# A Flamingo block on one core: key and value loads, the first normalisation and the shared FFN's matmul pieces moved in a hand-written order

## The reference

```python
x = x + tanh(g_xattn) * xattn(layernorm(x), ctx, ctx, W, b, mask)   # 16 heads of 16, causal and padding mask
z = layernorm(x)
shared = swiglu(z @ w_in.T) @ w_out.T                               # 256 -> 2 * 512 -> 256
# two groups of four experts: softmax over the groups, softmax in the best group, two best experts
h = swiglu(z @ w1.T)
routed = sum over experts e of (h * weight[:, e]) @ w2[e].T
x = x + tanh(g_ffn) * (shared + routed)
```

## Time and profile before

| | us |
|---|---|
| median of three runs | 1433.58 (1431.30 to 1433.97) |
| the profiled execution | 1430.63 |
| its span, first to last instruction | 1428.8 |
| mean granted TensorE clock | 0.929 of full speed |
| busy: TensorE, VectorE, GpSimd, ScalarE | 1201.9, 865.6, 552.0, 502.2 |

### The profile page before, as it was taken

The page is one execution under the profiler, slowest core; times in us unless marked ns, Lnnn a source line. Parts: engine busy times, 40 slices in busy tenths (PEclk is TensorE's granted clock), DMA queues, the critical chain, the costliest instruction groups (busy, mean ns, idle before and its releaser), DMA issues.

```text
span 1428.8 us, 22394 instructions
## 1 busy us (share of the span) xinstructions
PE 1201.9 (84%) x7387; PEld 953.1 (67%) x7387; DVE 865.6 (61%) x1968; ACT 502.2 (35%) x780; POOL 552.0 (39%) x658
## 2 busy tenths in 40 slices
PE   0577988888888888888888898626999999999997
PEld 0245766666666666666766666525888888888886
DVE  4435667466466567566466567773666666666665
ACT  3334434443444444444443443222222222222221
POOL 1112222422422422422522514354555656555543
PEclk9989999999999899999899899867999999999999
DMA  5466435445435335435435321343222222222210
GB/s 161 85 112 114 93 81 100 85 83 95 88 74 100 84 80 101 85 80 100 86 80 98 73 47 46 75 118 83 63 71 65 65 68 73 65 64 66 69 42 9
DMA packets 108263, 115.30 MB, mean 81 GB/s; under 512 B 36942, under 2 KB 88433, under 8 KB 108148
## 3 DMA queue, kind: packets, MB, share of 16 engines
q1 hardware_dynamic: 96376, 85.41, 29.1%
q0 software_dynamic: 11776, 28.46, 6.7%
HBM read 50.44 MB, written 28.64 MB: 55 GB/s over the span
## 4 chain that ended last, share of the span: by engine, by line
PE 57%; DVE 10%; DMA 8%; POOL 8%; issue 7%; SPq 5%; ACT 4%; POOLq 0%; ACTq 0%; DVEq 0%
PE ps L681 14%; PE ps L699 10%; DMA af<-in_ctxT 7%; PE ps L702 5%; PE ps L635 5%; PE ps L618 5%; POOL tab_dram L1375 3%; PE ps L541 3%; PE ps L526 3%; PE ps L550 3%; POOL gl L1358 2%; SPq L421 2%; PE ps L502 2%; PE ps L497 2%; PE ps L594 1%
## 5 line engine op out<-in xcount | busy, mean ns | idle before, releaser
L699 PE MATMUL ps<-w2a,gh 128*128 x608 | 218.7, 399 | 0.0
L702 PE MATMUL ps<-w2a,gl 128*128 x608 | 170.6, 281 | 0.0
L759 ACT ACTIVATE Pt<-ps,pbias 77x1024 f32<-77x1024 f32 x128 | 141.5, 1106 | 73.6 <-PE ps L528 73.1
L1358 POOL TENSOR_TENSOR gl<-gf,gh 128x512 fp32r<-128x512 f32 x64 | 82.6, 1290 | 148.1 <-ACT gh L801 148.1
L1303 POOL TENSOR_SCALAR ve<-mv 128x2 f32<-128x2 f32 x64 | 15.6, 244 | 317.0 <-DVE mv L882 316.4
L1411 POOL DMA_INDIRECT out<-ot,Pt x76 | 78.4, 1032 | 153.2 <-DVE ot L1232 149.7
L699 PEld LDWEIGHTS ps<-w2a,gh 128*128 128x128 f32 x608 | 114.3, 188 | 25.2
L681 PE MATMUL ps<-z2h,w1h 128*128 128x512 f32 x304 | 122.0, 401 | 7.4 <-DVE z2l L886 7.4
L618 PE MATMUL ps<-x2h,winh 128*128 128x512 f32 x256 | 124.3, 486 | 2.4 <-DVE gf L1157 1.5
L1093 DVE TENSOR_REDUCE mneg<-ps 128x8 f32<-128x616 f32 x128 | 101.6, 795 | 35.8 <-PE ps L502 35.7
L681 PE MATMUL ps<-z2l,w1h 128*128 128x512 f32 x304 | 121.1, 398 | 0.0
(11 more groups left out here) (205 smaller groups left out, 2858.7 us busy)
## 6 DMA issues: line engine op xcount, KB each, us to landing
w2a<-w2a SPq DMA_DIRECT2D x96, 256.0 KB, 5.8
af<-in_x SPq DMA_DIRECT2D x32, 256.0 KB, 4.1
x<-in_x SPq DMA_DIRECT2D x32, 256.0 KB, 7.0
y_dram<-xn SPq DMA_DIRECT2D x32, 256.0 KB, 3.5
y_dram<-res SPq DMA_DIRECT2D x32, 256.0 KB, 2.6
w2a<-w2a SPq DMA_DIRECT2D x96, 77.0 KB, 2.8
Pt<-in_w2T SPq DMA_DIRECT2D x16, 256.0 KB, 3.0
af<-in_ctxT SPq DMA_DIRECT2D x16, 154.0 KB, 6.8
```

The costliest lines, as they stand in the source:

```text
L699: e.matmul(o, gh2[:, c % 2, fc, t * P:(t + 1) * P], w2v[:, bass.ds(val, 1), fc, :, :].rearrange("p o h d -> p (o h) d"), start=fc == 0, st ...
L702: m = e.matmul(o[:, 0, :], gl2[:, c % 2, fc, t * P:(t + 1) * P], w2v[:, bass.ds(val, 1), fc, 0, :].rearrange("p o d -> p (o d)"), start=Fa ...
L759: e.activation(Pt[0:K, 4 * k:4 * k + 4, :].rearrange("k (n j) t -> k n (j t)", n=2), bank_of["sc", b, k][0:K, :, :], ACT.Exp, bias=pbias[: ...
L1358: e.tensor_tensor(gl[:, fc - 1, :], gf[:, n % 2, :], gh[:, fc - 1, :].bitcast(F), ALU.subtract).then_inc(s["gl"], 1)
```

## The change

Four edits of the order; no engine's code changes. The normalisation of block i + 1 leaves slot 11 of step i for slot 2 of its own step i + 1 (and the start of the list, for block 0). kv goes from slot 0 to slot 3 of the even step. load_kv for the next pair goes from the end of the odd step to slot 8 of the even step; load_x goes from behind slot 0 to behind slot 3. FFN pieces are put in two at a time, so a piece of even number stands one slot later, in the slot of the odd piece after it, and four route pieces follow in a slot where two followed.

```diff
     order += [("load_x", 0, 0), ("load_x", 1, 0), ("load_kv", 0, 0), ("own", 0, 0), ("moments", 0, 0),
-              ("norm", 0, 0), ("masks", 0, 0)]
+              ("masks", 0, 0)]
     for i in range(NB + 4):
...
-        put(i, ((7, "xT", 0), (10, "queries", 0)))
-        put(i + 1, ((8, "moments", 0), (11, "norm", 0)))
+        put(i, ((2, "norm", 0), (7, "xT", 0), (10, "queries", 0)))
+        put(i + 1, ((8, "moments", 0),))
         if i % 2 == 0 and i < NB:
-            slots[0].append(("kv", i // 2, 0))
+            slots[3].append(("kv", i // 2, 0))
+            if i + 2 < NB:
+                slots[8].append(("load_kv", i // 2 + 1, 0))
         for slot in range(12):
...
-            if slot == 0 and i + 2 < NB:
+            if slot == 3 and i + 2 < NB:
                 order.append(("load_x", i + 2, 0))
-            while at["ffn"] < 12 * (i - 5) + slot - 5:
+            while at["ffn"] < (12 * (i - 5) + slot - 5) // 2 * 2:
                 order.append(("ffn", at["ffn"] // 24, at["ffn"] % 24))
                 at["ffn"] += 1
                 for _ in range(2 if i < NB else 3):
                     route()
-        if i % 2 == 1 and i < NB - 1:
-            order.append(("load_kv", i // 2 + 1, 0))
```

## The result

The changed kernel takes 1311.23 us (median of four runs, 1309.0 to 1312.47) against 1432.44 us for the kernel before on the same chip: a ratio of 0.916 (95% interval 0.913 to 0.920). The forecast was 1335 us, range 1297 to 1385. The profiled execution took 1309.0 us, its span 1307.2 us, mean granted clock 0.969 (before 0.929).

A forecast was written before the change was run, and what follows sets the result against it. The prediction took the key-load stall, smaller odd-step gaps and slow clock after both as the bound; 84 us from 13 loads, 4.5 and 9 at the start, 97.5 us in all, gave 1335 us, range 1297 to 1385.

The forecast's parts named there:

- The key stall: ScalarE waits for keys, TensorE at L550 for its exponential; removal gains 7.2 us per plain pair, 4.6 per scatter pair.
- The wait for the maximum of quarter 2: TensorE's 0.90 us wait in plain pairs could vanish or reach about 1.7 us; 0.8 us more was charged.
- blocked routing operations: VectorE routing operations on two SBUF operands, held up beside GpSimd's subtraction, each cost about 1.1 us.
- The normalisation: Moving it from ScalarE's slot 11 to slot 2 gains 0.3 us per plain pair, 0.2 us per scatter pair.
- the 1.81 us gap: TensorE's wait at L635 in odd steps of plain pairs for GpSimd's L1358; 0.3 us of it taken back.
- The start: First steps: 4.5 us gained by normalisation after the weights, 9 us by two key loads before 134 us.
- The scatter pair: Scatters start some 2 us earlier; 2.3 of 3.34 us remain at L635, about 2 us gained with clock.
- The pairs of FFN pieces: Two FFN pieces at a time: quarter 1 scores lose cover against their maximum, costing some 0.3 us per pair.
- Odd gaps close too: Rival: the clock holds through the odd step, about 34 us beyond the forecast, 1301 us; chance 0.14.
- VectorE and GpSimd as the bound: Rival: more blocked routing pieces cost 26 us in plain pairs and 18 in scatter pairs, 1379 us; chance 0.18.
- The late row of maxima: Rival: SP's row, queued behind key copies and loads, comes 10.8 us late; about 1471 us, chance 0.04.
- The stall only moving: Rival: split-key copies land too late for the next step's maxima, TensorE waits there; about 1434 us, chance 0.04.

The follow-up runs named there:

- Experiment 1: The kernel before with load_kv for the next pair in slot 8 of the even step, kv still in slot 0: 1355.06 us, ratio 0.9458.
- experiment 4: The changed kernel with load_kv back at the end of the odd step, the split still in slot 3: 1307.49 us, ratio 0.9132.
- experiment 5: The changed kernel with keys and values split in slot 0 again, the load still ahead: 1302.12 us, ratio 0.9104.
- experiment 2: The kernel before with the first normalisation in slot 2 of its own step and load_x in slot 3: 1420.14 us, ratio 0.9899.
- experiment 3: The kernel before with FFN pieces put in two at a time: 1376.41 us, ratio 0.9600.
- experiment 6: The changed kernel with the first normalisation back in slot 11 of the step before: 1322.84 us, ratio 0.9245.
- experiment 7: The changed kernel with FFN pieces one to a slot again: 1344.89 us, ratio 0.9391.
- experiment 8: The changed kernel with FFN pieces still in pairs but all routing held back by one piece: 1338.52 us, ratio 0.9334.
- experiment 9: The changed kernel with load_kv in slot 11 of the even step, behind the row of maxima and the queries: 1310.09 us, ratio 0.9140.

## Why the prediction was right, and where it was wrong

The time came out 24 us below the forecast, inside its range. On the cuts used here the forecast splits so: three loads lie in the start, so 4.5 + 9 + 6.45 = 20 us there, and 12 x 6.45 = 77 us in the steady stretch. The start came out at 20.0 us, the steady stretch at 105.2 us. Nearly all of the miss is in the steady pairs. Worked out by the prediction's terms, about 48 us of the 77 were idle time and 30 us clock (2.5 us a pair); measured were 63.2 and 42.0 us.

By the waits of TensorE in the steady stretch, the idle part splits as follows (the prediction's terms for 12 pairs; 1.2 us more that it took for ScalarE's wait belong to no wait of TensorE):

| wait, change in us | forecast | measured |
|---|---|---|
| at L550 | -47.3 | -48.5 |
| at L635 | -8.0 | -24.1 |
| for VectorE's maxima | +8.4 | +0.6 |
| for the row of maxima, and at L541 | 0 | +8.6 |

- **The key stall: right in place, its size nearly.** Both waits of the earlier trace rows are gone. Experiment 1, which takes only that, gives 77 us (its term: six plain pairs at 7.2, seven others at 4.6, and 9 us at the start make 84). Its parts are further off than their sum: the steady stretch lost 55.3 us where 12 pairs make 71 (6.7 us at L550 stay for the routing exponential, the maxima cost 2.8 us more, and the clock gave back 18 us where 23 were counted), and the start lost 19.8 us where 14 to 16 were in the sum. The reason given was wrong in one point: I credited the 19 slots of lead, and said that without this cover 4.86 us come back. Experiments 4 and 5 show an early load or a late split to be enough, each without the other.
- **The wait for the maximum of quarter 2: taken at the wrong end.** I charged 0.8 us more; it fell from 0.90 to 0.28 us. The step that failed is the one on blocked routing operations. Before, two of them stood between VectorE's product and the maximum and both were held up; in the changed kernel these two run ahead of GpSimd's subtraction, and only one (L939) is caught beside it. VectorE before, then VectorE and GpSimd after:

```profile
416.98 1.28 DVE L935 TENSOR_TENSOR ge<-l,R 128x32 f32<-128x32 f32 x1
418.18 1.31 DVE L937 TENSOR_TENSOR c<-l 128x24 f32<-128x24 f32 x1
```

```profile
359.66 0.18 DVE L935 TENSOR_TENSOR ge<-l,R 128x32 f32<-128x32 f32 x1
359.76 0.18 DVE L937 TENSOR_TENSOR c<-l 128x24 f32<-128x24 f32 x1
...
361.23 1.29 DVE L939 TENSOR_TENSOR c<-l 128x16 f32<-128x16 f32 x1
...
361.19 1.29 POOL L1358 TENSOR_TENSOR gl<-gf,gh 128x512 fp32r<-128x512 f32 x1 [7.07 <-ACT gh L801]
```

- **The normalisation: the start right, the rest by luck.** At the start TensorE comes to its first wait for the maxima 4.5 us earlier (36.21 against 40.67 us), as forecast. The 0.3 us of the 1.81 us gap is there too (1.47 us are left), but it is not the normalisation's: experiment 2 leaves the gap at 1.8 us, experiment 3 alone brings it to 1.47, and experiment 6 keeps it there. The normalisation works in scatter pairs, where I gave it 0.2 us: it takes 0.9 us of that gap by itself (experiment 2), because GpSimd's last subtraction no longer stands for ScalarE (experiment 6).
- **The start: its 20 us were partly luck.** The load alone gives 19.8 us there, the normalisation alone 5.3. In the changed kernel the fourth block's scores wait 5.19 us for the row of maxima, where they waited 1.34.
- **The scatter pair: the term most mis-sized.** From the first scatter to the moment when TensorE is ready for piece 19 were 483.60 - 466.94 = 16.66 us, and are 422.28 - 403.86 = 18.42: the scatters start 1.76 us earlier against TensorE, the 2 us that I had worked out. But I let only 1 us of it count. And GpSimd's stretch from first scatter to piece 19 is 18.66 us and not 20.0, 0.8 of it by the wait for ScalarE that the normalisation's move took away. 3.34 - 1.76 - 1.34 = 0.24 us, the gap that is seen, where I left 2.3 us. In this pair TensorE is ready a little later than it could be, by the 0.36 us that it waited for the row of maxima. The slow stretch behind the gap went with it: TensorE's clock gave back 42.0 us in all where 30 were forecast.
- **The pairs of FFN pieces: wrong sign.** I charged 0.3 us a pair for lost cover and saw the routing's start as a detail of other terms. The wait of the scores for the maximum is there (0.37 us). But pairs are worth 34 us in the changed kernel and 57 us by themselves, and most of the 34 (27 by the medians of experiments 7 and 8) goes with the routing that starts one piece earlier. The routing exponential behind the key conversion, in the trace of before at 408.19 us, was in none of my rows.
- **The parts overlap.** Alone they give 77, 14 and 57 us, 148 in all, together 121. At L550 the load alone takes 41.8 us in the steady stretch and pairs alone 17.0, and only 48.5 stood there; at the start load and normalisation alone make 25 us, together 20.
- **The rivals.** "Odd gaps close too" (1301 us) came half true: nearly in scatter pairs, not in plain ones. VectorE and GpSimd as the bound: not seen; VectorE's busy time in the steady stretch is 437.67 us against 436.01, and of its routing operations six lasted over 1 us in two pairs before, four after. The late row of maxima came in small: 5.19 us once at the start and 2.87 us once in the steady stretch, both above the 2 us that the prediction named as a sign against it, with TensorE at 0.51 and 0.50 behind them, 17.9 us in all against 8.3 before; experiment 9 takes half of it away and gains nothing that can be measured. That the Trainium skill (DMA: Bandwidth & Descriptors, "Queues, rings and completion order") has descriptors consumed in ring order fits these two places, where load and row are issued back to back. But the load ahead is not enough for it: with the split in slot 0 the wait is 8.2 us (experiment 1) and 8.6 us (experiment 5), with the late split and no load ahead 10.6 us (experiment 4); only both together make 17.9 (15 to 17 in experiments 6 and 7). The stall only moving: no.

## What to carry to other kernels

In an order written by hand, ask of a small operation not only what it costs but which queue it stands in, and between which two others: a 0.2 us routing exponential held up a 1.1 us one that TensorE waited for, and moving the routing's start by one matmul piece was worth about a fifth of the whole gain (27 of 121 us, by holding it back). When a wait has two cures (fetch earlier, use later), try each alone: here either was enough, and the two together were no better than one. Cut the span at two marks that both kernels have, and split the difference into clock and idle time, before explaining it.

## What was not expected of the hardware

**Behind gaps of the same length the clock is sometimes down, sometimes not.** Windows from the end of a gap at L635, first in the changed kernel (1.47 and 1.48 us of idle time before), then in the kernel before (1.81 us in both):

```profile
376.07:381.00 4.93, 4.93 (x27) 4.57 (x28) 3.57 (x11) 0.86 (x2) 1.55 (x2) 0.65 0.85 216
467.48:472.40 4.92, 4.92 (x40) 4.49 (x40) 4.54 (x15) 1.98 (x3) 1.58 (x2) 1.00 0.91 219
```

```profile
433.29:438.70 5.41, 5.41 (x32) 5.10 (x32) 4.01 (x12) 0.07 (x1) 1.55 (x2) 0.68 0.86 207
542.05:547.40 5.35, 5.35 (x43) 4.74 (x43) 5.08 (x14) 1.59 (x2) 1.57 (x2) 1.00 0.91 211
```

In two of the four stretches the mean granted clock is between the two levels (in the first it is 0.51, 1.2 GHz, from 378.00 to 381.00 us), in the others 2.4 GHz throughout; 27 matmuls are recorded in the one, 40 in the other of after. What decides stays open.

**An operation with one tensor from SBUF was held up too.** In the kernel before, L983 (a TENSOR_SCALAR, mostly of 128x8) took 0.169 to 1.028 us, median 1.026; in the changed kernel never above 0.173. One of before:

```profile
432.23 1.02 DVE L983 TENSOR_SCALAR R<-R 128x8 f32<-128x8 f32 x1
```

It began 0.27 us into GpSimd's subtraction of the earlier trace rows and ended with it; that the one held up the other is read from these times and was not tested. The Trainium skill (SBUF — State Buffer, "SBUF: two separate sides") names, beside operations with two SBUF inputs, those in a two-port mode; whether L983 ran in such a mode no row here tells.

**The landing of one transfer.** The same 154 KB of keys land in 3.0 us (median) where the load is issued in slot 8, with a load of x right ahead of it in SyncE's queue; in 6.8 us behind the query copies at the end of the odd step, and in 6.7 us behind them in slot 11 (experiment 9).
